# Second experts: 39 tiles of 256 rows become 32 full slots and 7 half slots with weights of their own

## The reference, cut to what matters

```
gate_scores = softmax(x @ Wg)                       # 8 experts
topk_scores, topk_idx = top_k(gate_scores, 2)       # 4096 tokens, 8192 (token, expert) rows
topk_scores = topk_scores / (topk_scores.sum(-1) + 1e-08)
gate  = einsum("bsh,ehi->bsei", x, W11)             # 256 -> 512
value = einsum("bsh,ehi->bsei", x, W12)             # 256 -> 512
fused = gate * sigmoid(gate) * value
expert_out = einsum("bsei,eih->bseh", fused, W2)    # 512 -> 256
out = x + sum over the two experts of score * expert_out
```

## Time and profile before

| | us |
|---|---|
| median of 3 runs | 1127.42 (1127.01 to 1127.57) |
| the profiled execution | 1130.32 |
| its span, first to last instruction | 1128.6 |
| mean granted TensorE clock | 0.964 of full speed |

### The profile page before, as it was taken

The page is one execution under the profiler, slowest core; times in us unless marked ns, Lnnn a source line. Parts: engine busy times, 40 slices in busy tenths (PEclk is TensorE's granted clock), DMA queues, the critical chain, the costliest instruction groups (busy, mean ns, idle before and its releaser), DMA issues.

```text
span 1128.6 us, 25710 instructions
## 1 busy us (share of the span) xinstructions
PE 1052.6 (93%) x7884; PEld 981.6 (87%) x7884; DVE 736.1 (65%) x2273; ACT 675.2 (60%) x2491; POOL 523.5 (46%) x527
## 2 busy tenths in 40 slices
PE   6999999799999999889999999828999999999994
PEld 4688888699999999559999999728999999999994
DVE  6778885444444443857777777664777677766773
ACT  2788886444444443568999999614554455445451
POOL 1346776433333332335578887760343343333433
PEclk9999999899999999889999999868999999999997
DMA  9910001666666657201112221344748747398532
GB/s 318 337 61 25 29 30 47 235 203 227 225 226 230 224 186 237 76 10 38 39 62 77 72 72 61 138 165 153 241 65 251 242 107 201 66 341 252 138 61 29
DMA packets 91045, 163.53 MB, mean 145 GB/s; under 512 B 11858, under 2 KB 70100, under 8 KB 88532
## 3 DMA queue, kind: packets, MB, share of 16 engines
q1 hardware_dynamic: 72868, 134.07, 34.3%
q0 software_dynamic: 17376, 27.15, 11.5%
q10 hardware_dynamic: 720, 1.33, 0.3%
HBM read 159.46 MB, written 63.34 MB: 197 GB/s over the span
## 4 chain that ended last, share of the span: by engine, by line
PE 81%; DVE 6%; DMA 4%; issue 3%; ACT 3%; POOL 1%; SPq 1%; DVEq 0%; ACTq 0%; POOLq 0%
PE psum L1444 17%; PE psum L690 12%; PE psum L673 11%; PE psum L1155 10%; PE psum L1172 10%; PE psum L1429 8%; PE psum L645 3%; DMA E_up_w<-up 2%; PE psum L386 2%; ACT L_prob L740 2%; PE psum L696 2%; PE psum L1417 1%; PE psum L660 1%; DVE L_m_lo L438 1%; PE psum L349 1%
## 5 line engine op out<-in xcount | busy, mean ns | idle before, releaser
L1564 POOL DMA_INDIRECT out<-E_y,E_dest x78 | 126.2, 1618 | 234.8 <-DVE E_y L1527 110.8
L740 ACT ACTIVATE L_prob<-psum,L_neg_max 128x64 f32<-128x64 f32 x768 | 228.6, 362 | 4.6 <-DVE L_neg_max L973 4.6
L1444 PE MATMUL psum<-E_xT_hi,E_up_w 128*128 128x256 f32 x1248 | 224.0, 279 | 4.0 <-DVE E_xT_lo L1506 2.9
L1444 PEld LDWEIGHTS psum<-E_xT_hi,E_up_w 128*128 128x128 f32 x1248 | 192.7, 189 | 5.7 <-DVE E_xT_lo L1506 3.5
L740 ACT ACTIVATION_READ_ACCUMULATOR L_prob<-psum,L_neg_max 128x1 f32 x768 | 195.4, 257 | 0.0
L1444 PE MATMUL psum<-E_xT_lo,E_up_w 128*128 128x256 f32 x624 | 173.5, 278 | 0.0
L1481 ACT ACTIVATE E_sg<-psum 128x256 f32<-128x256 f32 x156 | 59.7, 383 | 161.1 <-PE psum L1444 159.0
L1444 PEld LDWEIGHTS psum<-E_xT_lo,E_up_w 128*128 128x128 f32 x624 | 117.7, 189 | 0.0
L690 PE MATMUL psum<-L_n_hi,L_pT_hi 128*128 128x256 f32 x384 | 109.0, 284 | 8.3 <-DVE L_pT_lo L980 8.3
L772 POOL TENSOR_TENSOR L_prob<-L_prob,L_rcp 128x512 f32<-128x512 f32 (+1 forms) x64 | 94.3, 1474 | 43.0 <-DVE L_rcp L939 41.5
L1213 ACT ACTIVATE E_h_hi<-psum 128x256 fp32r<-128x256 f32 (+1 forms) x128 | 55.7, 437 | 87.7 <-PE psum L1155 87.7
(11 more groups left out here) (200 smaller groups left out, 3101.6 us busy)
## 6 DMA issues: line engine op xcount, KB each, us to landing
E_up_w<-up SPq DMA_DIRECT2D x39, 2048.0 KB
E_w<-in_w SPq DMA_DIRECT2D x39, 512.0 KB
E_w<-in_w SPq DMA_DIRECT2D x16, 1024.0 KB, 7.5
E_xin<-rows SPq DMA_DIRECT2D x39, 260.0 KB
E_raw<-in_w SPq DMA_DIRECT2D x16, 512.0 KB, 6.9
up<-E_raw_hi SPq DMA_DIRECT2D x16, 512.0 KB, 5.8
up<-E_raw_lo SPq DMA_DIRECT2D x16, 512.0 KB, 3.8
rows<-zero SPq DMA_DIRECT2D x8, 640.0 KB, 14.4
```

What stands on the lines that cost most here:

```text
L740: last = e.activation(prob[q][:, h * KEYS:(h + 1) * KEYS], scores_ps(t)[:, h * KEYS:(h + 1) * KEYS], ACT.Exp, bias=nmx[:, q, h, :], accum_ ...
L1444: mm = q.matmul(bank, up_w[:, par, half, w, c, m * P:(m + 1) * P], x[:, c, :], start=(k == 0), stop=(k == 3 * KC - 1))
L1564: q.indirect_dma_start(p.out[:, :], bass.IndirectOffsetOnAxis(ap=dest[:, par, c, :], axis=0), y[:, par, c, :], None, compute_op=ALU.add).t ...
```

## The change

A tile becomes a slot. The plan counts each expert's rows in units of 128. Pairs of units go to NF = 32 full slots of 256 rows, computed as before; odd units, and pairs for which the 32 don't do, go to NH = 7 half slots of 128 rows. Slots that nobody needs are idle as before, full or half.

The loop body is now four full slots with one half slot between the third and the fourth; the last four full slots stand alone. A half slot has buffers, weights (`hup`, `hw2`) and semaphores of its own. ScalarE issues its two weight loads at the top of each body, always, with no condition. Its up products have the rows stationary and the weights moving, 12 products of 512 columns; the hidden rows then have to be transposed for the down products (`half_turn`, four transposes), of which there are 12.

At the start, expert 0's weights are now loaded ahead for slots 0 and 1 both. SyncE then makes conditional weight loads for both slots before it loads the rows of slots 0 and 1, and it waits for all eight tails ahead of them. The plan has 19 chained steps and more unchained ones.

```diff
-NT1 = (2 * TOK + E * (T1 - 1)) // T1
+NF, NH = 2 * TOK // T1, E - 1
+NT1 = NF + NH
+NP = NF + (NH + 1) // 2
...

...
-        c = Chain(q, s_tb, 0, 13)
+        need(q, s_pc, 7 + 2 * TC)
+        c = Chain(q, s_tb, 0, 19)
         c(q.tensor_tensor(t_a, p.next[:, 0, :], t_off[:, :], ALU.add))
...
+        q.tensor_scalar(p.tab[:, 0, 0:NF], first[:, 0:NF], float(IDLE_ROW), None, ALU.min)
+        q.tensor_scalar(p.tab[:, 0, NF:NT1], row_o[:, 0:NH], float(IDLE_ROW), None, ALU.min).then_inc(s_tab, 1)
         c.end()
...
-    def tiles_loop(eng, body):
-
-        body(0, 0, False)
-        body(1, 1, False)
-        with eng.Fori(1, NT1 // 2) as j:
-            body(2 * j, 0, False)
-            body(2 * j + 1, 1, False)
-        body(NT1 - 1, 0, True)
-    assert NT1 % 2 == 1
+    def slots(eng, body, last):
+
+        body(0)
+        with eng.Fori(1, NH) as j:
+            body(j)
+        last(4 * NH)
+    assert NF == 4 * (NH + 1)
...
+    def entry(q, row, i, top):
+        return q.value_load(p.tab[0:1, row, i:i + 1] if is_int(i) else p.tab[0:1, row, bass.ds(i, 1)], min_val=0, max_val=top)
+
     def first_weights(q):

         rows_from.need(q, rows_from.s_sim, NT)
-        q.dma_start(up_w[:, 0, :, :, :, :].rearrange("p j w c f -> p (j w c f)").bitcast(F32), up_d[0, :, :]).then_inc(s_w[0], 16)
-        q.dma_start(w2[:, 0, :, :], w2_d[:, 0, :, :]).then_inc(s_w2[0], 16)
+        for par in range(2):
+            q.dma_start(up_w[:, par, :, :, :, :].rearrange("p j w c f -> p (j w c f)").bitcast(F32),
+                        up_d[0, :, :]).then_inc(s_ahead, 16)
+            q.dma_start(w2[:, par, :, :], w2_d[:, 0, :, :]).then_inc(s_ahead, 16)

...
         def load_up(i, par):
-            e = expert(i)
-            new = None if is_int(i) and i < 2 else changed(i)
+            e = entry(q, 1, i, E - 1)
+            new = entry(q, 2, i, 1)
             wait(q, s_up, FC * (i - 1))
             land(q, i)
             q.dma_start(up_w[:, par, :, :, :, :].rearrange("p j w c f -> p (j w c f)").bitcast(F32),
                         up_d[e, :, :], cond=new).then_inc(s_w[par], 16)
...
+        def half_load_x(j):
+            r = entry(q, 0, NF + j, IDLE_ROW)
+            wait(q, sh_mt, NM * j)
+            wait(q, sh_xT, j)
+            land(q, j)
+            q.dma_start(hxin[:, :], d1[bass.ds(r, P), :]).then_inc(sh_x, 16)
+
+        def loads(i, par):
...
+        def body(j):
+            if not is_int(j):
+                loads(4 * j + 1, 1)
+            loads(4 * j + 2, 0)
+            half_load_x(j)
+            loads(4 * j + 3, 1)
+            loads(4 * j + 4, 0)
+
+        def last(a):
+            for k in range(1, 4):
+                loads(a + k, k % 2)
+        q.wait_ge(s_ahead, 16 * 4)
+        q.wait_ge(rows_from.s_tab, 2)
+        for i in range(2):
+            load_up(i, i)
+            load_w2(i, i)
+        q.wait_ge(rows_from.s_tab, 3)
         rows_from.rows_landed(q)
-        q.wait_ge(rows_from.s_tail0, 16)
-        q.dma_start(xin[:, 0, :, :], d1[0:T1, :].rearrange("(c p) d -> p c d", p=P)).then_inc(s_x[0], 16)
-        q.wait_ge(rows_from.s_tab, 2)
-        load_up(1, 1)
-        load_w2(1, 1)
         rows_from.tails_landed(q)
-        q.wait_ge(rows_from.s_tab, 3)
-        load_x(1, 1)
-
-        def body(i, par, last):
-            if not last and not (is_int(i) and i == 0):
-                load_x(i + 1, 1 - par)
-                load_up(i + 1, 1 - par)
-                load_w2(i + 1, 1 - par)
-        tiles_loop(q, body)
+        for i in range(2):
+            load_x(i, i)
+        slots(q, body, last)
...
+        def half_transposes(j):
+            q.wait_ge(sh_x, 16 * (j + 1))
+            q.wait_ge(s_xTlo, 4 * j + 3)
+            for kc in range(KC):
+                mm = q.transpose(ps[:, X_BANK + kc, 0:P], hxin[:, kc * P:(kc + 1) * P], p.ident[:, :])
+            mm.then_inc(sh_xT, 1)
+
+        def up(i, par, half=None):
...
+        def half_up(j):
+            q.wait_ge(sh_xTlo, j + 1)
+            q.wait_ge(sh_w, 16 * (j + 1))
+            for v in range(2):
+                q.wait_ge(s_hf, (4 * j + 2) * FC + v + 1)
+                k = 0
+                for c in range(KC):
+                    for w, x in ((0, hxT_hi), (0, hxT_lo), (1, hxT_hi)):
+                        mm = q.matmul(ps[:, UP_BANK + v, :], x[:, c, :], hup[:, v, w, c, :],
+                                      start=(k == 0), stop=(k == 3 * KC - 1))
+                        k += 1
+                mm.then_inc(sh_up, 1)
+
+        def half_turn(j):
+            q.wait_ge(sh_hf, j + 1)
+            q.wait_ge(s_hf, (4 * j + 2) * FC + 3)
+            for m in range(FC):
+                mm = q.transpose(ps[:, UP_BANK + 2, m * P:(m + 1) * P], hhf[:, m * P:(m + 1) * P], p.ident[:, :])
+            mm.then_inc(sh_hT, 1)
+
+        def down(i, par, half=None):
...
+        def half_down(j):
+            q.wait_ge(sh_w2lo, j + 1)
+            q.wait_ge(sh_hlo, j + 1)
+            q.wait_ge(s_y, TC * (4 * j + 2) + 1)
+            k = 0
...
+        def body(j):
+            a = 4 * j
+            up(a, 0)
+            transposes(a + 1, 1)
+            if not is_int(j):
+                down(a - 1, 1, j - 1)
+            up(a + 1, 1)
+            transposes(a + 2, 0)
+            down(a, 0)
+            up(a + 2, 0)
+            half_transposes(j)
+            down(a + 1, 1)
+            half_up(j)
+            transposes(a + 3, 1, j)
+            down(a + 2, 0)
+            half_turn(j)
+            up(a + 3, 1, j)
+            transposes(a + 4, 0)
+            half_down(j)
+
...
+        def half_loads(j):
+
+            e = entry(q, 1, NF + j, E - 1)
+            wait(q, sh_up, 2 * j)
+            land(q, j)
+            q.dma_start(hup[:, :, :, :, :].rearrange("p j w c f -> p (j w c f)").bitcast(F32), up_d[e, :, :]).then_inc(sh_w, 16)
+            wait(q, sh_w2lo, j)
+            land(q, j)
+            q.dma_start(hw2[:, :, :], w2_d[:, e, :, :]).then_inc(sh_w2, 16)
+
...
+        def half(j):
+            q.wait_ge(sh_up, 2 * j + 1)
+            wait(q, sh_hf, j)
+            q.activation(hsg[:, :], ps[:, UP_BANK, :], ACT.Silu).then_inc(sh_sg, 1)
+            q.wait_ge(sh_w2, 16 * (j + 1))
+            wait(q, sh_dn, j)
+            q.activation(hw2_hi[:, :, :], hw2[:, :, :], ACT.Copy).then_inc(sh_w2hi, 1)
+            split_x(4 * j + 3, 1)
+            q.wait_ge(sh_hT, j + 1)
+            q.activation(hT_hi[:, :, :].rearrange("p m t -> p (m t)"), ps[:, UP_BANK + 2, :], ACT.Copy).then_inc(sh_hhi, 1)
+
+        def body(j):
+            a = 4 * j
+            half_loads(j)
+            full(a, 0, lambda: split_x(a + 1, 1))
+            full(a + 1, 1, lambda: split_x(a + 2, 0))
+            full(a + 2, 0, lambda: half_split_x(j))
+            half(j)
...
+        def half(j):
+            q.wait_ge(sh_up, 2 * j + 2)
+            q.wait_ge(sh_sg, j + 1)
+            wait(q, sh_hT, j)
+            q.tensor_tensor(hhf[:, :], ps[:, UP_BANK + 1, :], hsg[:, :], ALU.mult).then_inc(sh_hf, 1)
+            split_x(4 * j + 3, 1)
+            half_meta(j).more(NM)
+            q.wait_ge(sh_w2hi, j + 1)
+            q.tensor_tensor(hw2_lo[:, :, :], hw2[:, :, :], hw2_hi[:, :, :].bitcast(F32), ALU.subtract).then_inc(sh_w2lo, 1)
+            outputs(4 * j + 2, 0)
+            q.wait_ge(sh_hhi, j + 1)
+            wait(q, sh_dn, j)
+            q.tensor_tensor(hT_lo[:, :, :].rearrange("p m t -> p (m t)"), ps[:, UP_BANK + 2, :],
+                            hT_hi[:, :, :].rearrange("p m t -> p (m t)").bitcast(F32), ALU.subtract).then_inc(sh_hlo, 1)
+            q.wait_ge(sh_mt, NM * (j + 1))
+            wait(q, sh_add, 16 * j)
+            q.tensor_copy(hdest[:, :], hmb[:, :])
+
+        def body(j):
+            a = 4 * j
+            full(a, 0, lambda: split_x(a + 1, 1), lambda: None if is_int(j) else outputs(a - 1, 1))
+            full(a + 1, 1, lambda: split_x(a + 2, 0), lambda: outputs(a, 0))
+            full(a + 2, 0, lambda: half_split_x(j), lambda: outputs(a + 1, 1))
+            half(j)
+            full(a + 3, 1, lambda: split_x(a + 4, 0), lambda: half_outputs(j))
...
+        def half_add(j):
+            q.wait_ge(s_add, 16 * TC * (4 * j + 3))
+            q.wait_ge(sh_y, j + 1)
+            land(q, j)
+            q.indirect_dma_start(p.out[:, :], bass.IndirectOffsetOnAxis(ap=hdest[:, :], axis=0),
+                                 hy[:, :], None, compute_op=ALU.add).then_inc(sh_add, 16)
+
+        def body(j):
+            a = 4 * j
+            if not is_int(j):
+                add(a - 1, 1, j - 1)
+            add(a, 0)
+            add(a + 1, 1)
+            add(a + 2, 0)
+            half_add(j)
```

More of the change, by code:

```diff
@@ L1475, in hidden_hi, with full @@
             q.activation(h_hi[:, par, m, :], hf[:, m, :], ACT.Copy).then_inc(s_hhi, 1)
-        def body(i, par, last):
+        def full(i, par, behind):
             for m in range(FC):
@@ L1485, in body, with last @@
                     hidden_hi(i, par, m - 1)
-            if not last:
```

(33 more changed lines are left out.)

217 lines of the change are left out of this document (143 added, 74 removed).

## The result

The changed kernel takes 1142.08 us (median of 4 runs, 1140.96 to 1143.38) against 1127.49 for the kernel before (4 runs, 1127.01 to 1130.66). The ratio is 1.0124, with a 95% interval of 1.0102 to 1.0146: **slower by 1.2%**, though it computes seven half slots where there were seven whole tiles. The profiled execution of the changed kernel took 1141.39 us. Two executions further down (one of e8's ten, 1127.19 us, and one of e13's six, 1705.47 us with a mean granted clock of 0.555) are slow ones, which the medians include and the ratios leave out.

A forecast was written before the change was run, and what follows sets the result against it. TensorE's work, plus what makes it wait, was taken as the bound. Terms -26.6 + 22.2 + 1.5 + 6.4 + 7.5 + 3.5 = +14.5 us put the median at 1142 us, range 1116 to 1149.

The forecast's parts named there:

- TensorE's work: Second experts' stage: seven tiles of 8.62 us become half slots of 4.83 us, -26.6 us.
- the signs: What the profile would show, including 300 to 310 us of PE work up to the last product.
- the bound of one wait: Per collision: 1.3 us if the half load were free, 6.3 if all 4.9 us fall on it.
- The four collisions: Slots 5, 9, 13, 25: half and full weight loads run at once, waits of 5.8 us each, +22.2 us net.
- U: End of slot 4j-1's up products, the time from which issues, landings and slot 4j+1's due time are counted.
- Second slots: Slots 10, 14, 26: their own loads queue late behind others, 0.5 us each, +1.5 us (0 to 5).
- The clock: Lower granted clock behind the four waits, 1.6 us each, +6.4 us (0 to 12).
- The start: Second stage's start: four weight calls ahead of row tile 0 delay it, +7.5 us (3 to 10).
- Half slots and VectorE: Half slots: VectorE runs late, split rows late by 0.5 us seven times, +3.5 us (0 to 14).
- A: Rival: half loads are hidden, four waits of only 1.3 us, clock holds; faster, 1116 us; chance 0.24.
- B: Rival: VectorE becomes the bound in the half slots, all seven stall 2 us more; 1156 us; chance 0.08.
- C: Rival: collisions happen lightly, waits of 4 us without clock loss; 1127 us, no change; chance 0.09.

The follow-up runs named there:

- e8: Changed kernel with half weights issued by SyncE behind slot 4j+2, only where the owner changes, and slot 0's rows loaded first; 1120.66 us.
- e13: Changed kernel, half loads on ScalarE inside slot 4j only where the expert differs, slot 0's rows first, four buffers for scaled rows; 1122.52 us.
- e1: Changed kernel, but half slots 1 to 6 load no weights and compute with half slot 0's (wrong results); 1112.64 us.
- e3: Changed kernel with ScalarE issuing the half weights one slot later, behind its work for slot 4j; 1140.62 us.
- e11: Changed kernel with ScalarE issuing the half weights inside slot 4j, behind its first Silu, instead of ahead of the slot; 1139.47 us.
- e4: Changed kernel with SyncE loading slot 0's rows before the four conditional weight calls; 1138.91 us.
- e6: Changed kernel with half slots 1 to 6 loading weights only where the owner differs from the half slot before; 1120.49 us.

## Why the prediction was right

1142.0 was forecast, 1142.08 came, and by the steps that it named; the exactness is luck, as the parts below show. For the profiled executions they give +14.5 by the forecast and +16.2 as measured, and the attention, which no term touched, took some 6 us off again in that profile. The range of 1116 to 1149 took in a faster kernel as well as a slower one.

- **TensorE's work, -26.6.** Right. A half slot has 0.22 + 2.80 + 0.44 + 1.38 = 4.84 us in the chain above (the last is `half_down`), forecast 4.83. PE's work up to the last product was misjudged elsewhere, in the signs: 300 to 310 us are given and 329.9 were busy; the 343.1 busy us of before less 26.6 are 316.5, and slower products add to it. Two slips are too small to matter: 7 times 3.79 is 26.5, and the bound of one wait is 6.2.
- **The four collisions, +22.2.** Right in place, cause and nearly in size: waits of 5.1, 5.4, 5.1 and 5.2 us where 5.8 was forecast, at slots 5, 9, 13 and 25. For slot 5, U is 809.3: the half load went out at U+2.3, the full one at U+3.2 (3.1), landed at U+16.3 (16.5), and slot 5 was due at U+11.3 (10.7). e1 shows the cause, e3 that the place decides. The share of 4 to 4.9 us for the bytes of the other load held: 8.95 became 13.1 to 13.5.
- **Second slots, +1.5.** Wrong: 0.7 at slot 18 and nothing at 10, 14 and 26. The first slot's wait gives the queue the time back. e11 shows the other side: take the wait from the first slot and the second has it.
- **The clock, +6.4.** Too small: 8.7. I took the 4 us at 0.57 of the earlier trace rows for the whole dip; at these waits it is 6.8 us at 0.50, of which 4.1 to 6.1 lie behind the wait.
- **The start, +7.5.** Right as a sum: the first product was forecast 6.7 us later and came 6.9 to 7.2 later, the slower first slot was forecast at 0.8 and cost 0.4. Some 3 us of it vary with the tail stores, so part of this is luck. The split is incomplete: under the weight calls lay the landing of all eight tails, which I had put down as hidden, and which e4 uncovers. The first product came at 770.07 and not near 775 because the attention ended sooner.
- **Half slots and VectorE, +3.5.** The waits are 0.25 in six of seven bodies and not 0.5, 1.5 in all; some 4 us of slower pace that no step named fill the rest and more, and their cause is open.
- **Rivals.** A (the loads are hidden) falls with e1. It was right that the DMA engines are far from full over the stage, 0.70; at the place itself the share is 1.00. B falls: no VectorE wait in the half slots. C falls with the clock.

## What to carry to other kernels

A load that is needed much later is not free if it is issued beside one that is due: 2 MB of half weights with 20 us to spare delayed by 4 us, four times, a load with none, and each of the four waits cost 2.2 us more through TensorE's clock. Look up the DMA share in the 10 to 15 us around the tightest load and not the mean of the stage, and put the patient load in the queue of the urgent one, where nothing is due behind it. Moving it by a slot or by two microseconds mostly moved the wait (1140.62 and 1139.47 us). Not loading what is there already, with this routing four of six loads, gained 21.6 us, the better place 15.5.

## What the runs showed of the hardware that was not expected

- At each idle spell of 5.1 to 5.4 us in the kernel after, the granted clock was 0.50 for 6.8 us. In e11, where the waits came in pieces of 1.3 to 2.7 us, stretches of 3.4 us at 0.50 stood behind the later pieces, at slots 6, 10, 14 and 18, and none behind the others. In e6 a wait of 3.0 us had 6.8 us at the lower level and one of 3.5 us had 3.4, so the longer wait does not always cost more.
- An indirect add of 128 rows has a median of 3.8 us from issue to landing. GpSimd's `half_add` had one of 11.8 in the kernel after, where four of the seven were in flight beside two loads of 2 MB, and of 8.0 in e1, where only SyncE's loads ran.
- The end of the attention moved from 746.7 to 751.6 us between executions with the same code up to there, and went with the granted clock of the 220 us ahead of 700: 0.98 for the late ones, 0.99 or 1.00 for the early ones.
